# Values of 48 of 50 token tiles by seven block products per pair of tiles, key norms applied on ScalarE, block sums on GpSimd

## The reference, cut to what matters

```python
# cross_attention_states: 6404 x 512;  Wk, Wv: 1024 x 512 (8 heads of 128)
k = (cross_attention_states @ Wk.T).reshape(bsz, kv_len, KVH, HD).transpose(0, 2, 1, 3)
v = (cross_attention_states @ Wv.T).reshape(bsz, kv_len, KVH, HD).transpose(0, 2, 1, 3)
...
k = _rmsnorm(k, k_norm_w)      # per key and head: k * rsqrt(mean(k*k) + 1e-5) * w
# and, in the first block, for each of the 1024 rows of s (1376 wide):
_, idx = jax.lax.top_k(-jnp.abs(s), k)      # the 688 smallest magnitudes are set to 0
```

## Time and profile before

| | us |
|---|---|
| median of 3 runs (2704.76 to 2705.18) | 2705.08 |
| time of the profiled execution | 2704.6 |
| its span | 2702.8 |
| PE, DVE, ACT, POOL busy in the span | 2686.3, 2158.0, 1445.4, 1093.4 |
| keys and values on PE | from 127.5 to 717.7 of the span |

### The profile page before, as it was taken

How to read it: one execution, slowest core, us unless ns; L and a number is a source line. 1 busy time by engine, 2 the same in 40 slices (tenths; PEclk the granted TensorE clock), 3 DMA queues, 4 the chain that set the end, 5 groups by cost and what they waited for, 6 DMA issues and landing times.

```text
span 2702.8 us, 46815 instructions
## 1 busy us (share of the span) xinstructions
PE 2686.3 (99%) x14580; PEld 2334.5 (86%) x14580; DVE 2158.0 (80%) x3264; ACT 1445.4 (53%) x3134; POOL 1093.4 (40%) x1016
## 2 busy tenths in 40 slices
PE   9999999999999999999999999999999999999999
PEld 8888888888888888888888888888888888888887
DVE  5789999999855568888888888888888888887644
ACT  3234333433424456666666666666666666666421
POOL 0132222223313356555555555555555555554000
PEclk9999999999999999999999999999999999999999
DMA  6453334333333442121211112121211112112632
GB/s 216 134 180 109 113 109 116 109 110 112 121 125 113 128 152 79 58 65 58 65 58 46 60 58 65 58 65 58 65 58 55 55 54 65 58 45 90 188 109 75
DMA packets 260399, 246.70 MB, mean 91 GB/s; under 512 B 13200, under 2 KB 215696, under 8 KB 260336
## 3 DMA queue, kind: packets, MB, share of 16 engines
q1 hardware_dynamic: 260336, 245.92, 29.5%
HBM read 150.03 MB, written 95.85 MB: 91 GB/s over the span
## 4 chain that ended last, share of the span: by engine, by line
PE 98%; issue 1%; DVE 0%; ACT 0%; POOL 0%; DMA 0%; SPq 0%; POOLq 0%; DVEq 0%; ACTq 0%
PE banks L158 27%; PE banks L159 27%; PE banks L160 27%; PE banks L1894 13%; PE banks L388 2%; PE banks L1401 1%; PE banks L1911 1%; PE banks L1909 1%; PE banks L1120 0%; PE banks L2247 0%; DMA x_raw<-xT_in 0%; PE banks L1142 0%; PE banks L2237 0%; DVE p_odd L1802 0%; POOL p_odd L1661 0%
## 5 line engine op out<-in xcount | busy, mean ns | idle before, releaser
L1850 DVE TENSOR_TENSOR pT_lo<-banks,pT_hi 128x512 fp32r<-128x512 f32 (+1 forms) x832 | 573.0, 689 | 93.2 <-ACT pT_hi L1769 80.9
L1769 ACT CAST pT_hi<-banks 128x512 fp32r<-128x512 f32 x576 | 334.7, 581 | 404.9 <-PE banks L1894 404.7
L723 DVE TENSOR_SCALAR_CACHE_REDUCE flags<-abs_s,cand 128x1376 bf16<-128x1376 f32 x248 | 393.2, 1642 | 1.2 <-DVE cand L740 0.2
L158 PE MATMUL banks<-k_hi,q_hi 128*128 128x416 f32 (+1 forms) x1024 | 374.4, 366 | 1.2 <-DVE t_min L1802 1.2
L159 PE MATMUL banks<-k_lo,q_hi 128*128 128x416 f32 (+1 forms) x1024 | 353.0, 345 | 0.0
L160 PE MATMUL banks<-k_hi,q_lo 128*128 128x416 f32 (+1 forms) x1024 | 351.2, 343 | 0.0
L158 PE MATMUL banks<-pT_hi,v_hi 128*128 128x512 f32 x768 | 344.2, 448 | 0.0
L158 PE MATMUL banks<-kvw_hi,c_hi 128*128 128x512 f32 x800 | 316.1, 395 | 0.0
L1802 DVE CUSTOM_DVE_ANT_0 p_odd<-banks,minus_mask 128x1664 f32<-128x1664 f32 x128 | 242.1, 1891 | 89.3 <-PE banks L160 89.3
L160 PE MATMUL banks<-kvw_hi,c_lo 128*128 128x512 f32 x800 | 312.1, 390 | 0.0
L1661 POOL TENSOR_SCALAR p_even<-p_even,p_inv 128x1601 f32<-128x1601 f32 x127 | 205.5, 1618 | 262.0 <-DVE p_inv L1809 261.8
(11 more groups left out here) (206 smaller groups left out, 5615.4 us busy)
## 6 DMA issues: line engine op xcount, KB each, us to landing
raw<-keys SPq DMA_DIRECT2D x32, 800.5 KB, 4.5
values<-v_sb SPq DMA_DIRECT2D x50, 512.0 KB, 2.6
keys<-kT_sb SPq DMA_DIRECT2D x50, 512.0 KB, 4.8
raw<-values SPq DMA_DIRECT2D x32, 768.0 KB
queries<-qT_sb SPq DMA_DIRECT2D x64, 256.0 KB, 2.6
raw<-queries SPq DMA_DIRECT2D x32, 512.0 KB, 5.2
attended<-o_sb SPq DMA_DIRECT2D x128, 128.0 KB, 1.9
raw<-attended SPq DMA_DIRECT2D x64, 256.0 KB, 2.9
```

The costliest lines, as they stand in the source:

```text
L158: pe.matmul(out, a_hi, b_hi, start=start, stop=False)
L723: bits.done(dve.tensor_scalar(flags[:, tt % 2], abs_s[:, tt], at[:, tt:tt + 1].bitcast(F32), 0.0, ALU.is_lt, ALU.add, accum_out=out[:, tt: ...
L1769: act.copy(pT_hi[:, m % RING], t_bank(m)).then_inc(pT_hi_act, 1)
L1850: dve.tensor_tensor(pT_lo[r, m % RING], t_bank(m)[r], pT_hi[r, m % RING].bitcast(F32), ALU.subtract).then_inc(pT_lo_done, 1)
```

## The change

The last two tiles keep the old form. For the other 48, the values of two tiles (2a, 2a+1) are one product of a 2 x 2 block matrix (two tiles by two halves of the contraction) with a 2 x 2 block matrix (two halves of the contraction by two halves of the columns), by Strassen's scheme in the form with fifteen sums: seven block products of 6 matmuls each in place of eight. Around it:

- the sums of weights, t_sum (T1 to T4, both halves of the contraction), are made once: one half on VectorE, one on GpSimd; 14 weight pieces are split in place of 8;
- the sums of context blocks, s_sum (S1 to S4), are made on GpSimd for each pair (`sum_c`, four instructions of 128 x 256), and split on ScalarE and GpSimd (`split_s`);
- the seven products leave PSUM by seven ScalarE copies of 128 x 512 (`take`), and GpSimd adds them (`add`, five of 128 x 512 for each pair; two more sums are accumulated in PSUM);
- the keys are scaled by `rstd` on ScalarE, eight instructions of 128 x 128 for a tile, in place of one on VectorE;
- VectorE's search runs without the key instructions in between;
- keys have two pairs of PSUM banks in turn, not three;
- u, s_lo, flags and order lie in the `raw` buffer, so the loads for the down projection are issued behind the last pair.

One window of the new code handles one pair: TensorE computes products P1, P6, P7, transposes tile 2a, computes P5, P2, P4, P3, transposes tile 2a+1, then the keys of tiles 2a+2 and 2a+3.

```diff
 def key_banks(chip, s):
-    first = (0, 4, 2)[s]
+    first = (0, 4)[s % 2]
...
     def gpsimd(pool):
...
+        def window(i, s):
+            p = pair(i, s)
+            root(i, s + 1)
+            pool.wait_ge(v_sb_done, copied(p, P6_SB))
+            add(u[:, 0], u[:, 0], u[:, 1])
+            pool.wait_ge(u_sum_done, u_sum(p, U2))
+            pool.wait_ge(v_sb_done, copied(p, P7_SB))
+            add(u[:, 1], u[:, 0], u[:, 1])
+            if not is_last(i, s):
+                pool.wait_ge(s_lo_done, s_lo_at(p, 1))
+                sum_c(i, s + 2)
+            pool.wait_ge(u_sum_done, u_sum(p, U3))
+            pool.wait_ge(v_sb_done, copied(p, P5_SB))
+            add(v_sb[:, 1, right], u[:, 1], v_sb[:, 1, right])
+            pool.wait_ge(v_sb_done, copied(p, P4_SB))
+            add(v_sb[:, 1, left], u[:, 0], v_sb[:, 1, left])
+            split_c(i, s + 3)
+            pool.wait_ge(v_sb_done, copied(p, P3_SB))
+            add(v_sb[:, 0, right], u[:, 0], v_sb[:, 0, right])
+            if not is_last(i, s):
+                split_s(p + 1)
+                split_c(i, s + 4)
+            root(i, s + 2)
...
     def scalar(act):
+        def norm_keys(i, s):
+            t = BODY * i + s
+            act.wait_ge(rstd_done, done(t))
+            act.wait_ge(kT_done, done(t - 1))
+            for g in range(G):
+                at = slice(g * HD, (g + 1) * HD)
+                last = act.activation(k_sb[:, at], k_banks(s)[:, at], ACT.Copy, scale=rstd[:, s % RING, g:g + 1])
+            last.then_inc(k_sb_done, 1)
...
+        def window(i, s):
+            p = pair(i, s)
+            squares(i, s + 1)
+            act.wait_ge(u_sum_done, u_sum(p, 0))
+            take(p, P1, u[:, 0], a_ps)
+            take(p, P6, u[:, 1], b_ps)
+            act.wait_ge(u_sum_done, u_sum(p, U2))
+            take(p, P7, u[:, 1], e_ps)
+            norm_keys(i, s + 1)
...
+            take(p, P5, v_sb[:, 1, right], d_ps)
+            turned(i, s)
...
+            take(p, P2, v_sb[:, 0, left], a_ps)
+            take(p, P4, v_sb[:, 1, left], e_ps)
+            take(p, P3, v_sb[:, 0, right], d_ps)
...
+            squares(i, s + 2)
+            norm_keys(i, s + 2)
...
     def tensor(pe):
+        def window(i, s):
...
+            pe.wait_ge(v_sb_done, copied(p, 0))
+            wait_weights(1)
+            times(a_ps, *a11, B11, True)
+            wait_weights(2)
+            pe.wait_ge(s_lo_done, s_lo_at(p, 1))
+            times(b_ps, *s2, T2, True)
+            wait_weights(3)
+            times(e_ps, *s3, T3, True)
+            transpose_keys(pe, chip, k_sb, BODY * i, s)
+            wait_weights(4)
+            times(d_ps, *s1, T1, True)
+            wait_weights(5)
+            pe.wait_ge(v_sb_done, copied(p, P1_SB))
+            times(a_ps, *a12, B21, False)
+            wait_weights(6)
+            pe.wait_ge(v_sb_done, copied(p, P7_SB))
+            times(e_ps, *a22, T4, False)
+            wait_weights(7)
+            pe.wait_ge(v_sb_done, copied(p, P5_SB))
+            times(d_ps, *s4, B22, False)
+            transpose_keys(pe, chip, k_sb, BODY * i, s + 1)
+            keys(i, s + 2)
+            if not is_last(i, s):
+                keys(i, s + 3)
...
     def sync(sp):
+        pairs(sp, window)
+        sp.wait_ge(v_done, product_done(PAIRS, 0))
+        sp.wait_ge(w_lo_done, CHUNKS + 2 * PRODUCTS + 2)
...
+        down.early["first_loads"](sp)
```

More of the change, by code:

```diff
@@ L552, in keys_and_values @@
+    v_bank = 6
     v_ps = psum[:, v_bank:v_bank + NB, :].rearrange("p b n -> p (b n)")
+    left, right = slice(0, 512), slice(512, N)
     BODY = 2 * RING
-    TRIPS = STEPS // 2
+    TRIPS = PAIRS // RING - 1
     LAST = KT - 1
[L558 to L564, removed]
+    assert KT == 2 * PAIRS + 2 and PAIRS % RING == 0
@@ L691, in scalar @@
+        split_c(0, 2)
+        squares(0, 0)
         for s in range(2):
             act.wait_ge(sem(f"p_out{s}"), landed(TT // 2 - 1))
-        tiles(act, step, TRIPS, LAST)
+        norm_keys(0, 0)
+        pairs(act, window)
         i, s = LAST // BODY, LAST % BODY
+        act.wait_ge(v_out[0], landed(PAIRS - 1))
+        act.wait_ge(v_done, done(PRODUCTS * PAIRS))
+        act.copy(v_sb[:, 0], v_ps).then_inc(v_sb_done, 1)
+        turned(i, s - 1)
         squares(i, s)
@@ L799, in vector @@
         down.early["split_gates"](dve, 0, 0)
[L800 to L803 removed]
+        dve.wait_ge(rstd_done, done(LAST))
+        dve.wait_ge(kT_done, done(LAST - 1))
+        dve.tensor_tensor(k_sb[:].rearrange("p (g d) -> p g d", g=G),
+                          k_banks(LAST).rearrange("p (g d) -> p g d", g=G),
+                          rstd[:, LAST % RING].unsqueeze(2).to_broadcast((P, G, HD)), ALU.mult
+                          ).then_inc(k_sb_done, 1)
@@ new lines, in tensor, with keys, times, window @@
+    def tensor(pe):
+        def keys(i, s, first=False):
+            pe.wait_ge(c_lo_done, done(BODY * i + s))
+            pe.wait_ge(kT_sb_done, done(BODY * i + s - 2))
+            out = k_banks(s)
+            for j in range(NB):
+                for c in range(CT):
+                    if first:
+                        pe.wait_ge(w_lo_done, CT * j + c + 1)
+                    last = product(pe, out[:, j * 512:(j + 1) * 512], c_hi[s % RING][:, c], c_lo[s % RING][:, c],
+                                   k_hi[:, j, c], k_lo[:, j, c], c == 0, c == CT - 1)
+            last.then_inc(k_done, 1)
+        def times(out, a_hi, a_lo, blk, start):
+            for k in range(2):
+                hi, lo = vw[:, blk, 0, k], vw[:, blk, 1, k]
+                for n, (a, b) in enumerate(((a_hi, hi), (a_hi, lo), (a_lo, hi))):
+                    last = pe.matmul(out, a[:, k], b, start=start and k + n == 0, stop=k == 1 and n == 2,
+                                     skip_group_check=not start)
+            last.then_inc(v_done, 1)
+        def window(i, s):
+            p = pair(i, s)
+            upper, lower = s % RING, (s + 1) % RING
+            a11, a12 = ((c_hi[upper][:, at], c_lo[upper][:, at]) for at in (slice(0, 2), slice(2, 4)))
+            a22 = c_hi[lower][:, 2:4], c_lo[lower][:, 2:4]
+            s1, s2, s3, s4 = ((s_hi[:, n], s_lo[:, n]) for n in range(4))
+            def wait_weights(n):
+                pe.wait_ge(w_lo_done, CHUNKS + 2 * n)
+            pe.wait_ge(v_sb_done, copied(p, 0))
[20 more added lines that the diff above has]
+            keys(i, s + 2)
+            if not is_last(i, s):
+                keys(i, s + 3)
+        def values(i, s, blocks):
@@ L817, in values @@
-        def values(i, s, first=False):
-            pe.wait_ge(v_sb_done, done(BODY * i + s - 1))
-            project(i, s, 1, v_ps, range(NB), first).then_inc(v_done, 1)
-        def step(i, s):
-            keys(i, s + 1)
-            transpose_keys(pe, chip, k_sb, BODY * i, s)
-            values(i, s + 1)
+                    blk, k = ((B11, B21), (B12, B22))[j][c // 2], c % 2
+                    last = product(pe, v_ps[:, j * 512:(j + 1) * 512], c_hi[s % RING][:, c], c_lo[s % RING][:, c],
+                                   vw[:, blk, 0, k], vw[:, blk, 1, k], c == 0, c == CT - 1)
```

393 lines of the change are left out of this document (253 added, 140 removed).

## The result

The changed kernel takes 2767.19 us (median of 4 runs, 2766.49 to 2769.05), the kernel before 2705.1: a ratio of 1.0231, with an interval from 1.0219 to 1.0244. 62 us slower, where 2763 was forecast. The profiled execution has a span of 2765.0 us.

What follows compares the result with a forecast made beforehand. TensorE was taken to bound the kernel before, and a path across engines the changed windows. Windows -4, first window +20, selection +38 and end +4 make +58 on 2704.6: 2763 us, range 2718 to 2790.

Steps and rivals of the forecast that it cites:

- TensorE's own work: Keys and values stage: a window with TensorE never idle lasts 22.24 us, 23.6 less the 1.36 of six saved matmuls.
- The ring: Path through a window over ScalarE, GpSimd and TensorE: 23.4 us, above TensorE's 22.24; 22 windows give -4 us.
- The scaling: Key scaling on ScalarE in each window: 0.26 us per instruction, 2.2 a tile; 0.16 and 1.4 if the scalar cost nothing.
- The first window: Start of the keys and values stage: sums, splits and scaling delay its end from 161.9 to 182.6, +20 us.
- Reach across it nowhere: First window: VectorE's 18 sums and splits run beside GpSimd's work without holding it up.
- The selection: choose on VectorE, from 587 us within the windows: it and GpSimd block each other, +38 us, bounds 0 and 58.
- The deductions of 10, 6 and 4: Taken from choose's 58.1 us: 10 in GpSimd's idle time, 6 for blocked starts, 4 beside the powers' compute part.
- The end: Before the down projection: its loads wait for the last pair's last product, so gates and weights come late, +4 us.
- Selection absorbed: Rival: VectorE's and GpSimd's instructions fall beside each other without loss, 2725 us; chance 0.13.
- this rival's second half: Selection absorbed and scalings of 1.4 us as well: windows of 22.7, 20 us gained, 2705 us, no change; chance 0.05.
- TensorE the bound in each window: Rival: window path below 22.24 us and a selection costing under 4 give a faster kernel, 2696 us; chance 0.04.
- Clock: Rival: TensorE's clock falls to 1.2 GHz in its new pauses, +23 us over three windows, 2786 us; chance 0.10.

Runs made afterwards that it cites:

- the run with both orders: Changed kernel with ScalarE copying P5 before scaling the second tile's keys, and GpSimd making the next pair's first root before the last add and split: 2742.90 us.
- GpSimd's order alone: Changed kernel with only GpSimd's root of tile 2a+2 moved before the last sum and the split of tile 2a+4: 2765.10 us.
- Copy P5 first: Changed kernel with only ScalarE's copy of P5 moved before its scaling of the second tile's keys: 2765.88 us.
- the run with counts: Changed kernel with the 32 choose instructions replaced by 35 counts that take VectorE as long, selection left out: 2728.78 us.
- choose's first form: Changed kernel with the 32 choose instructions replaced by 61 comparisons of one tile operand against a column, selection left out: 2750.48 us.
- the two runs with counts: 35 counts for choose, once in the changed kernel (2728.78 us), once in that with P5 copied earlier, GpSimd's root earlier and tile 0 scaled early (2704.68 us).
- the run with the early start: Changed kernel with P5 copied earlier, GpSimd's root earlier, and tile 0's squares, root and scaling ahead of the block sums' splits: 2740.71 us.

## Why the prediction was right

**TensorE's own work, 22.24 a window:** 22.22 in the run with both orders.

**The ring, 23.4:** 23.27 (23.25 with GpSimd's order alone), through the instructions listed. Over 22 windows it gained 7 us against two tiles of 11.79 on the timeline before, not 4. What the step missed is the second ring. I had counted GpSimd's 18.4 us as filling time, "up to 0.6 late" at one place. Its line in the profile is 18.4 of work, 4.46 of waiting for squares, and 0.77 for a copy: 23.6, less the overlaps of neighbours. The number did not suffer; advice from it would have. "Copy P5 first" was worth 20 us by the prediction's ring and 1.3 on the chip.

**The scaling, 0.26 each and 2.2 a tile:** 2.17 in both kernels, 0.25 from start to start. The 293 ns that the prediction estimates from the page "ScalarE: Activation LUTs" of the Trainium skill (What ACT_TABLE_LOAD costs) would make 2.3; the trace does not agree with it.

**The first window, +20:** its end is at 186.1, not 182.6, so +24.2. This is the term whose size was most off. GpSimd's starting line was longer than its rows from before: four powers 8.56 for 7.31, the low part of tile 2 3.42 for 1.3, as VectorE's sums and splits ran beside them.

```profile
131.53 8.56 POOL L474 TENSOR_TENSOR rest_rstd<-rest_var,minus_half 128x8 f32<-128x8 f32 x4 [2.83 <-DVE rest_var L464]
...
156.33 3.42 POOL L725 TENSOR_TENSOR c_lo<-c_raw,c_hi 128x512 fp32r<-128x512 f32 x1 [4.27 <-ACT c_hi L818]
```

"Reach across it nowhere" was the sentence that failed: the mechanism of the earlier trace rows was applied to the selection and not to the start.

**The selection, +38, from 587:** the price is 36.8 by the trace and 38.4 by the run with counts. The place was wrong: it runs from 652.8 to 728.4. The search took 15.5 us a bit, not 13.5, because its four small instructions wait for GpSimd as well (below). The windows that it met were of the same kind, so the price held. The deductions of 10, 6 and 4 from VectorE's 58 were not measured one by one, and 57 us of choose's first form, which the prediction did not tell from the other three, cost 21.7: that the total came so close is in part luck.

**The end, +4:** waits of 4.8 and 0.5.

**Sum:** 24.2 - 7 + 36.8 + 5.3 = 59, and the spans differ by 62.2. Of the 3 us between, 1.2 are the first six matmuls of the down projection, which run at the lower clock behind the wait of 4.8 (2.70 from 777.27 to 779.97, before 1.47). The other 1.8 lie in the attention, which the change does not touch: from the first to the last transposition of `p_even` it is 1467.3 before, 1469.1 here and 1467.3 in the run with counts.

**The rivals.** Selection absorbed: excluded by the two runs with counts (38.4 less in one, 36.0 less than the run with the early start in the other). The time of this rival's second half was summed wrongly: a ring of 22.7 gains 20 in place of the 4 that the 2725 already holds, which makes 2709, not 2705. TensorE the bound in each window: not in this kernel, but it takes two edits of order to get there.

Clock: it does fall in the pauses (0.82, 0.74 and 0.86 of full in the rows above, and eight transposes at 164.15 take 1.97 instead of 1.04, the lower level, 1.2 GHz). The run with counts has 1.00 from 670 to 700, so there the fall follows from the pauses. But the rival's price did not come, since TensorE is not what the path runs through where its clock is low. In the three long windows GpSimd waits as in a window in the middle (4.46 for squares, 0.77 for the copy ahead of its second add), and nowhere else:

```profile
699.01 0.53 POOL L731 TENSOR_SCALAR var<-ssq 128x8 f32<-128x8 f32 x1 [4.46 <-ACT square L831]
```

So all of the 36.8 is the length of GpSimd's own instructions. In the first window P5, at the lower clock, is over by 168.5, and ScalarE copies it at 172.12, behind the scaling and without a wait; up to there the path is GpSimd's and ScalarE's. What is left for the clock is the 1.2 at the end.

## What to carry to other kernels

Work moved to an engine with idle time is free only if it is on no ring: write down the line of every engine through one period, the mover's too, with its waits. Where one edit of order brings nothing, look for a second ring of the same length before you give the first up. On engines that exclude one another, add their times, less what still overlaps, instead of comparing them, and ask whether the saving is needed in the stretch where both are busy: taking 3 of 24 pairs back to plain products, reckoned at 4 us, brought 37 in all against the run of 2740.71 (3 of them from the earlier loads: the wait at the end fell from 7.6 to 4.3).

## What was unexpected of the hardware

Small instructions of VectorE wait for GpSimd too. The search's four instructions on 128 x 8 elements, groups of the changed kernel from 127 to 800 us (busy us, mean ns):

```profile
L957 DVE TENSOR_TENSOR cand<-thr,bit 128x8 uint32<-128x8 uint32 x31 | 26.9, 867 | 1.7 <-DVE thr L965 0.7
L963 DVE TENSOR_SCALAR below<-less 128x8 uint32<-128x8 f32 x31 | 21.1, 682 | 1.1
...
L965 DVE COPY_PREDICATED thr<-below,cand 128x8 uint32<-128x8 uint32 x31 | 20.1, 647 | 4.7 <-DVE below L963 4.6
...
L961 DVE TENSOR_SCALAR bit<-bit 128x8 uint32<-128x8 uint32 x31 | 15.9, 513 | 0.0
```

Before, the means were 163, 172, 171 and 166 ns. Those of the search's first bit end when the GpSimd instruction beside them does (the first below at 172.99, GpSimd's at 172.96), and where GpSimd pauses (185.2 to 189.6) the same instruction takes its usual time:

```profile
172.24 0.72 POOL L742 TENSOR_TENSOR s_sum<-c_raw 128x256 f32<-128x256 f32 x1
...
172.34 0.65 DVE L961 TENSOR_SCALAR bit<-bit 128x8 uint32<-128x8 uint32 x1
...
188.32 0.17 DVE L961 TENSOR_SCALAR bit<-bit 128x8 uint32<-128x8 uint32 x1
```

So 124 instructions of 0.17 us lost 63 us to a neighbour that they barely touch, while 248 counts of 1.64 us beside them lost nothing. That is what moved the selection from 587 to 652.
